# Minus the maxima written into the score banks by ScalarE, in place of a product of two rows

## The reference

```
c_q = h @ w_down_q.T
c_kv = h @ w_down_kv.T
q, k, v = up projections, split into 16 heads; q and k rotated
scores = einsum('bhqd,bhkd->bhqk', q, k) * scale
attn = softmax(scores, axis=-1)
out = einsum('bhqk,bhkd->bhqd', attn, v)
out = out @ w_out.T + residual
```

## Time and profile before

| | us |
|---|---|
| median of 3 timed runs | 900.91 |
| lowest and highest | 897.12, 901.8 |
| the profiled execution | 895.69 |
| its span, first to last instruction | 894.0 |
| busy in it: TensorE, GpSimd, VectorE, ScalarE | 813.2, 662.7, 637.1, 397.2 |
| mean granted TensorE clock | 0.963 |

### The profile page before, as it was taken

How to read it: one execution, slowest core, us unless ns; L and a number is a source line. 1 busy time by engine, 2 the same in 40 slices (tenths; PEclk the granted TensorE clock), 3 DMA queues, 4 the chain that set the end, 5 groups by cost and what they waited for, 6 DMA issues and landing times.

```text
span 894.0 us, 14690 instructions
## 1 busy us (share of the span) xinstructions
PE 813.2 (91%) x5118; PEld 485.9 (54%) x5118; DVE 637.1 (71%) x1156; ACT 397.2 (44%) x650; POOL 662.7 (74%) x348
## 2 busy tenths in 40 slices
PE   4689999999999999999999999999999977968581
PEld 2445555555555555555555555555555444368581
DVE  8987777777777777777777777777776757646022
ACT  3654444444444444444444444444444433336340
POOL 2579998898987878787878787878777856632333
PEclk8979999999999999999999999999999999969796
DMA  9101001010101011111011111101010000078683
GB/s 246 31 1 14 13 14 25 14 25 13 25 13 26 13 26 14 27 20 26 6 26 25 22 25 14 24 14 14 13 13 15 12 13 1 19 238 269 213 314 89
DMA packets 84330, 43.91 MB, mean 49 GB/s; under 512 B 57632, under 2 KB 73376, under 8 KB 84192
## 3 DMA queue, kind: packets, MB, share of 16 engines
q1 hardware_dynamic: 83232, 40.86, 18.2%
q0 software_dynamic: 1024, 2.10, 0.7%
HBM read 36.51 MB, written 6.16 MB: 48 GB/s over the span
## 4 chain that ended last, share of the span: by engine, by line
PE 82%; DVE 8%; DMA 4%; POOL 2%; issue 2%; ACT 1%; POOLq 0%; SPq 0%; DVEq 0%
PE ps_o L456 25%; PE ps_m L422 9%; PE ps_x L410 8%; PE ps_s L440 7%; PE ps_s L442 6%; PE ps_s L446 6%; PE ps_s L444 6%; PE ps_s L473 3%; DMA moe<-xs_dram 3%; PE ps_s L464 3%; PE ps_s L595 2%; PE ps_s L586 2%; POOL xs_dram L953 2%; DVE mx L1097 1%; PE ps_s L377 1%
## 5 line engine op out<-in xcount | busy, mean ns | idle before, releaser
L939 POOL TENSOR_TENSOR acc<-acc,probs 128x1024 f32<-128x1024 f32 (+1 forms) x192 | 459.9, 2395 | 74.7 <-ACT probs L697 52.5
L1097 DVE TENSOR_REDUCE mx<-ps_m 128x2 f32<-128x1024 f32 x240 | 293.7, 1224 | 90.9 <-PE ps_m L422 90.3
L697 ACT ACTIVATE probs<-ps_s 128x1024 f32<-128x1024 f32 x256 | 248.8, 1024 | 157.7 <-PE ps_s L446 157.6
L456 PE MATMUL ps_o<-probs,c_all 128*64 128x512 f32 x1024 | 249.5, 608 | 0.0
L440 PE MATMUL ps_s<-q_hi,k_hi 64*128 64x512 f32 x512 | 102.6, 397 | 12.0 <-DVE x_sb L1153 12.0
L456 PEld LDWEIGHTS ps_o<-probs,c_all 128*64 128x64 f32 x1024 | 62.4, 136 | 93.2 <-issue 44.5
L422 PE MATMUL ps_m<-k_hi,q_hi 64*128 64x512 f32 x480 | 107.7, 444 | 4.0 <-DVE mx L1097 4.0
L939 POOL TENSOR_TENSOR acc<-probs 128x1024 f32<-128x1024 f32 (+1 forms) x32 | 75.4, 2357 | 48.3 <-ACT probs L697 47.8
L442 PE MATMUL ps_s<-q_hi,k_lo 64*128 64x512 f32 x512 | 101.4, 391 | 0.0
L446 PE MATMUL ps_s<-neg_row,one_row 64*128 64x512 f32 x512 | 101.3, 391 | 0.0
L444 PE MATMUL ps_s<-q_lo,k_hi 64*128 64x512 f32 x512 | 100.8, 389 | 0.0
(11 more groups left out here) (299 smaller groups left out, 1025.5 us busy)
## 6 DMA issues: line engine op xcount, KB each, us to landing
probs<-in_experts SPq DMA_DIRECT2D x15, 578.0 KB, 6.0
rr<-rd_dram SPq DMA_DIRECT2D x62, 128.0 KB, 3.1
wu<-in_wqk SPq DMA_DIRECT2D x16, 256.0 KB, 3.4
neg_row<-nm SPq DMA_DIRECT2D x256, 0.5 KB, 2.0
w_first<-in_experts SPq DMA_DIRECT2D x5, 578.0 KB, 5.2
rot<-in_experts SPq DMA_DIRECT2D x5, 578.0 KB, 5.0
hT<-in_experts SPq DMA_DIRECT2D x5, 578.0 KB, 5.6
xs_dram<-zero SPq DMA_DIRECT2D x2, 960.0 KB, 9.4
```

What stands on the lines that cost most here:

```text
L456: ins = nc.tensor.matmul(ps_o[64 * h:64 * h + 64, :], c_all[:, (p // HP) * TB + kt, :], probs[:, st % 4, h, :], start=(kt == 0), stop=(kt ...
L697: nc.scalar.activation(probs[:, st % 4, :, :], ps_s[:, 2 * (st % 2):2 * (st % 2) + 2, :], ACT.Exp, scale=SCALE).then_inc(s["probs"], 1)
L939: V.tensor_tensor(acc[:, half, heads, :], first, probs[:, st % 4, heads, :], ALU.add).then_inc(s["added"], 1)
L1097: V.reduce_max(mx[:, :, kh, qt], max_banks(q, n), AX.X).then_inc(s["max_reduced"], 1)
```

## The change

ScalarE writes minus the maxima into a step's two banks before its scores (`preset`), and the three remaining products add to what stands there (`start=False`). The row product, `one_row` and `neg_row` go. For this the maxima must stand on all partitions: SP stores `nm` to DRAM in one DMA per half pair (`mr_dram`, four numbers of one partition together) and reads it back as a row, copied to all 128 partitions, with one DMA per head (`neg_wide`). In that row query `t*128 + p` stands at place `4*p + t`, so ScalarE, which writes the bank in order of queries, reads with a step of four numbers, 16 bytes. There are two copies of the row per head, one for each half.

The preset of steps `2g+2` and `2g+3` follows the exponentials of group `g`. Step 9 and the next pair's step 1 come after the denominators' copy; these two write bank 2 and bank 3 by themselves, since bank 3 waits for the outputs to be added. On TensorE a step's scores wait for `preset` alone, and in groups 3 and 7 the denominators and outputs stand between the value products of the two steps. The outputs' four products into one bank now clear its accumulation marks once. The spreading DMAs are placed on SP between a store of the reciprocals and its read back.

```diff
-        one_row = sb("one_row", [P, P], F32R)
-        neg_row = sb("neg_row", [P, 2, S], F32R)
+        neg_wide = sb("neg_wide", [P, 2, 2, HALF])
...
-                ge(pe, s["probs"], n_step(p, st) - 2)
-                if kt == 0:
-                    pe.wait_ge(row_placed[half], 128 * (p + 1))
-                if kt == 1:
-                    ge(pe, s["den_read"], n_part(p, half) - 2)
-                    ge(pe, s["out_added"], n_part(p, half) - 3)
+                pe.wait_ge(s["preset"], n_step(p, st))
...
-                for h in range(2):
-                    ins = nc.tensor.matmul(bank[h], one_row[rows(h), :], neg_row[rows(h), p % 2, qc], start=False, stop=True)
...
-                                           g_all[:, p // HP, p % HP, :], start=True, stop=True)
+                                           g_all[:, p // HP, p % HP, :], start=(n == 0), stop=(n == 3))
...
-                    for n in (2 * g - 2, 2 * g - 1):
+                    def value_step(n):
...
+                    value_step(2 * g - 2)
                     if g in (3, 7):
                         pe.wait_ge(s["probs"], n_step(p, 2 * g + 1))
...
+                    value_step(2 * g - 1)
...
+            wide_rows = lambda half: neg_wide[:, half, :, :].rearrange("a h (p t) -> a h t p", t=4)
+            wide_row = lambda half, h: neg_wide[:, half, h, :].rearrange("a (p t) -> a t p", t=4)
+            bank = lambda n: ps_s[:, n, :].rearrange("a (t p) -> a t p", t=4)
+            banks = lambda n, k: ps_s[:, n:n + k, :].rearrange("a h (t p) -> a h t p", t=4)
+
+            def preset(p, st):
+
+                half, kt = divmod(st, TB)
+                if p == 0 and st < 2:
+                    act.wait_ge(s["max_reduced"], NMAX - 1 + st)
+                ge(act, s["probs"], n_step(p, st) - 2)
+                if kt == 0:
+                    act.wait_ge(row_wide[half], 32 * (p + 1))
+                if kt == 1 and (p or half):
+                    ge(act, s["den_read"], n_part(p, half) - 2)
+                    nc.scalar.copy(bank(2), wide_row(half, 0))
+                    ge(act, s["out_added"], n_part(p, half) - 3)
+                    nc.scalar.copy(bank(3), wide_row(half, 1)).then_inc(s["preset"], 1)
+                else:
+                    nc.scalar.copy(banks(2 * (st % 2), 2), wide_rows(half)).then_inc(s["preset"], 1)
...
+                    if g < NGRP - 1:
+                        preset(p, 2 * g + 2)
+                        if g != 3:
+                            preset(p, 2 * g + 3)
+                    elif p < LAST:
+                        preset(p + 1, 0)
...
+                sp.dma_start(mr_dram[half].rearrange("h (p f) -> p h f", f=4), nm[:, half, :, :]).then_inc(row_out[half], 16)
+
+            def max_spread(q, half):
+
+                sp.wait_ge(row_out[half], 16 * (q + 1))
+                if q:
+                    sp.wait_ge(s["preset"], n_step(q - 1, TB * half + TB - 1))
                 for h in range(2):
...
+                    sp.dma_start(neg_wide[:, half, h, :],
+                                 mr_dram[half, h:h + 1, :].to_broadcast([P, HALF])).then_inc(row_wide[half], 16)
```

More of the change, by code:

```diff
@@ L211, in build @@
             "max_row": "both heads' maxima of half the queries, negated (vector)",
-            "scores": "both heads' scores of a step, less the maximum (tensor)",
+            "preset": "a step's score banks hold minus the maximum (scalar)",
+            "scores": "both heads' scores of a step, added to it (tensor)",
             "probs": "their probabilities (scalar)",
@@ L250, in build @@
         up_in = sem("up_in")
-        row_placed = [sem(f"row_placed{n}") for n in range(2)]
+        row_out = [sem(f"row_out{n}") for n in range(2)]
+        row_wide = [sem(f"row_wide{n}") for n in range(2)]
         den_cols_in, inv_out, inv_in = sem("den_cols_in"), sem("inv_out"), sem("inv_in")
@@ L760, in exp_logits @@
                 nc.scalar.activation(rt[b][:, 1, :], rt[b][:, 0, :], ACT.Exp).then_inc(s["logit_exp"], 1)
+            preset(0, 0)
+            preset(0, 1)
             for p in range(NPAIR):
@@ L765, in _ @@
                         den_out(p - 1, 0, ps_s[:, 2, :])
+                        preset(p, 1)
                     if g == 4 and p > 0:
                         den_out(p - 1, 1, ps_s[:, 2, :])
+                    if g == 4:
+                        preset(p, 9)
                     if g == 6 and p == LAST:
@@ L1004, in then @@
                 dve.wait_ge(s["vector_step"], seq[0])
[L1006 to L1010 removed]
+            V.memset(ones[:], 1.0).then_inc(s["constants"], 1)
             def statistics(src, tiles):
@@ L1100, in neg_max @@
                 dve.wait_ge(s["max_reduced"], NMAX * q + TB * (half + 1))
-                ge(dve, row_placed[half], 128 * q)
+                ge(dve, row_out[half], 16 * q)
                 V.tensor_reduce(nm[:, half, :, :], mx[:, :, :, 4 * half:4 * half + 4].rearrange("p h k t -> p h t k"),
@@ L1378, in max_rows @@
                 sp.wait_ge(s["max_row"], 2 * q + half + 1)
-                if q >= 2:
-                    sp.wait_ge(s["scores"], n_step(q - 2, TB * half + TB - 1))
+                sp.dma_start(mr_dram[half].rearrange("h (p f) -> p h f", f=4), nm[:, half, :, :]).then_inc(row_out[half], 16)
[3 more added lines that the diff above has]
+                    sp.wait_ge(s["preset"], n_step(q - 1, TB * half + TB - 1))
                 for h in range(2):
-                    for n in range(4):
-                        row = neg_row[64 * h:64 * h + 1, q % 2, half * HALF + n * P:half * HALF + (n + 1) * P]
-                        sp.dma_start(row.bitcast(F32), nm[:, half, h, n:n + 1].bitcast(F32)).then_inc(row_placed[half], 16)
+                    sp.dma_start(neg_wide[:, half, h, :],
+                                 mr_dram[half, h:h + 1, :].to_broadcast([P, HALF])).then_inc(row_wide[half], 16)
             def den_cols(p, half):
@@ L1430, in _ @@
             weights(2)
-            sp.wait_ge(s["constants"], 1)
-            max_rows(0, 0)
-            max_rows(0, 1)
+            for half in range(2):
+                max_rows(0, half)
+                max_spread(0, half)
             weights(3)
@@ L1447, in _ @@
                     inv_rows(p - 1, 1)
+                if p < LAST:
+                    max_spread(p + 1, 0)
+                if p > 0:
                     inv_spread(p - 1, 1)
```

18 lines of the change are left out of this document (7 added, 11 removed).

## The result

The changed kernel takes 1007.09 us (median of four runs, 1004.38 to 1009.89) against 899.01 for the kernel before (896.12 to 901.8, four runs on the same chip): a ratio of 1.120, 95% interval 1.115 to 1.126. Experiments ran on several chips, which differ by some 0.6%, so across them the text compares ratios to the kernel before on the same chip, and stretches of the traces. In one of them, the store in the queries' order, two of the four runs took up to 2.5% longer at a lower granted clock (0.92), and only the other two are used.

A forecast was written before the change was run, and what follows sets the result against it. TensorE was taken to bound the kernel. Removed products -58.9, maxima wait +25.2, last pair +3.7, seam +2.0 and start +1.5 gave -26.5 us, from 900.91 to 874; own range 861 to 888, with rivals 860 to 992.

The forecast's parts named there:

- Why I take none: ScalarE's read of the row: only even distances between 16-byte pieces cost, so a 16-byte step, always odd, is free.
- the 0.98 of the sum: Time taken for one ScalarE preset of 128x1024 into two banks, within bounds of 0.97 to 1.09 us without the step.
- The half-rate rival: Each preset costs 0.85 us more, ScalarE becomes the bound, TensorE waits; +87, 988 us; chance 0.34.
- Its price for the groups with denominators: Half-rate rival's ScalarE time in groups with denominators: 6.9 us against 7.0, counted as -3.
- The slack: ScalarE's chain per group: the next exponential is due at 6.01, the cast ends at 5.51, so 0.5 us spare.
- the point from which a preset would cost: ScalarE's presets: no gain left from 0.25 us extra each, and the kernel slower from about 0.43.
- The maxima wait: TensorE's second maxima product can't start before 1.92 us after the first: 0.21 us in 120 groups, 25.2 us given back.
- the forecast for a free step: ScalarE's 16-byte step costs nothing and the maxima are late: -26.5 us, 874 us; chance 0.52.
- The start: Two presets stand before the first score: 1.5 us by the 0.98 each, less the wait there is.

The follow-up runs named there:

- The copies alone: Separate kernel without attention, only copies and reductions at various steps; ScalarE's 128x512 copy from SBUF took 0.59 us in order, 1.06 with 16 bytes.
- the kernels with cheap presets: Changed kernel with row and bank in order (885.2 us, 0.987), the step moved to the bank (891.3, 0.986), or stores in 8-byte pieces (887.59, 0.990).
- the kernel with the value step between: Kernel before without the row product, with a value step between the two steps' scores and the second maxima product: 924.42 us, ratio 1.031.

## Why the prediction was wrong

**The step that failed** is "Why I take none", the price of the 16 bytes. It rested on three rare reductions. What they cost I had read nearly right: 0.83 and 0.66 ns per element for 32 and 60 bytes, where reductions alone, of 512 elements, lose 0.74 and 0.63 (1.07 and 1.01 us against 0.69). Wrong was what I made of it, a cost that depends on whether the distance is even or odd and so is none at 16 bytes. The copies alone show no such thing: every step from 16 to 64 bytes that was run costs a ScalarE copy 0.42 to 0.48 us per 512 elements, and in the kernel a preset took 2.06 us for the 0.98 of the sum. The half-rate rival, which I gave 0.34, was the right mechanism: ScalarE the bound, TensorE waiting for presets, 50.7 us a pair where it had 49. The rule of the Trainium skill that I set aside ("SBUF — State Buffer", Specifications: two hits on each piece of 16 bytes for full rate) forecast it, and the runs agree: two hits (8 bytes) 0.61 us, one hit (16 bytes) 1.06.

**The rival's size** was off too, and with it the range. I carried over VectorE's extra per element as if it were ScalarE's: 1.83 us for a preset as an upper bound. What the two share is the time of a stepped read, not the extra; ScalarE, being faster in order, loses more. A preset takes 2.06 on the page and 1.95 from start to start, so two are 0.24 us above the rival's 3.66; but the exponentials go at 1.82 from start to start, not 1.94, and a plain group is 5.98, only 0.10 above its 5.88. Its price for the groups with denominators, 6.9, was right (393.92 to 400.86 in the trace). What it left out is the copy of the sums, 0.48 us in two groups of a pair: with ScalarE full it adds 1.0 us to each pair, and 50.7 is 49 with these two. It also took pair 0 as one like the others, 5 us longer than before; from first exponential to first exponential it went from 40.2 to 51.0.

**The slack** of 0.5 us per group, and with it the point from which a preset would cost, was about right: 0.30 more per preset moved the time by some 5 us only.

**The maxima wait** was right where it was placed (1.91 us measured, 1.92 forecast), and short by the 0.11 us that the up projection starts later behind it: 120 x 0.11 = 13 us. That is most of the distance between the forecast for a free step, 26.5 us of gain, and the 9 to 13 that the kernels with cheap presets bring: with the copies in order a middle pair takes 43.2 us, for 44.2 before and 42.2 forecast. The rest is at the ends: pairs 0 and 1 gained nothing (40.1 and 44.5 us, 40.2 and 44.5 before), and the last two took 94.7 together for 92.7.

The weight loads show where the 0.11 stands. Those of the second maxima product, in the kernel before and in the one without the row product:

```profile
316.64 0.19 PEld L422 LDWEIGHTS ps_m<-k_hi,q_hi 64*128 64x128 f32 x2
```

```profile
355.38 0.22 PEld L422 LDWEIGHTS ps_m<-k_hi,q_hi 64*128 64x128 f32 x2 [0.43 <-issue]
```

The first begins 0.23 us ahead of its product (316.87), the second 0.03 ahead (355.41). Between 150 and 650 us the kernel before has 87 such products with the load ahead and the up projection 0.31 to 0.34 behind them, and four without, three of those at 0.43; the kernel without the row product has 93, all with the load beside the product and the up projection 0.42 to 0.44 behind. So the 0.11 goes with a load that isn't ahead. A wait is not the only thing that it stands with: behind a value step, without a wait, it is 0.43 too (320.52 to 320.95 in the kernel with the value step between). What keeps the load back was not tested by itself.

**The parts that cost nothing** held together: with the copies in order the changed kernel runs at the ratio of the kernel that merely lacks the product. The start was 3.7 us later (the first exponentials at 70.56 after 66.82), where I had 1.5; but the kernels with cheap presets have them anywhere from 65.0 to 70.97, so a single trace can't tell what the presets did there.

## What to carry to other kernels

A reading of three rare rows is no price: where a change hangs on a cost that no row shows, give the written rule for it at least the chance of one's own theory, and carry over from another engine the time of the operation, not the surcharge. When data must be permuted between SBUF and PSUM, let the side in PSUM have the step. And before a group is made shorter on the bounding engine, list what it waits for next, the phase of VectorE's SBUF-only operations against GpSimd's among it.

## What the runs showed of the hardware that I had not expected

- SBUF reads with a step, 512 elements of four bytes: 8 bytes all but free (0.61 and 0.69 us on ScalarE and VectorE, 0.59 and 0.69 in order), 12 bytes 0.83 on both, 16 to 64 bytes 1.01 to 1.07 on both. PSUM with 16 bytes, read or written by ScalarE: 0.59, as in order.
- A weight load of 64x128 with a step of 16 bytes takes 306 ns instead of 184.
- VectorE's product of two SBUF inputs ends 0.37 us after the GpSimd addition that was running at its start; beside back-to-back additions it took 2.86 us for 0.69 of work.
- The value products cost 0.15 us more per group when they are cut in two pieces of four.
- A maxima product whose weights are not loaded ahead has the up projection 0.11 us later behind it (0.43 against 0.32 us).
